# Attention and mixture-of-experts block on one core: down products turned round, transposes on VectorE, preparation jobs in other slots

## Chip, core and metric

One NeuronCore of a Trainium2 chip runs the whole kernel as a single program. The metric is the device time of one execution in microseconds (us). Three executions of the kernel before gave 531.87, 533.58 and 533.83 us, a median of 533.58 us.

## What is computed

`x` and `ctx` are 4 batches of 512 tokens with 256 features, all float32.

```python
x = x + tanh(g_xattn) * xattn(layernorm(x), ctx, ctx)     # 16 heads of 64, rope, window of 64
x = x + tanh(g_ffn)   * ffn(layernorm(x))

def ffn(x, shared_up, shared_down, routed_up, routed_down, router_w):
    up_s   = einsum('th,seh->tse', xt, shared_up)                  # 2 shared experts, 128 wide
    shared = einsum('tse,she->th', gelu(up_s), shared_down)
    probs  = softmax(xt @ router_w.T)                              # 16 routed experts
    topk_p, topk_i = top_k(probs, 4)
    gate   = zeros_like(probs).at[arange, topk_i].add(topk_p)
    up_r   = einsum('th,reh->tre', xt, routed_up)
    act    = gelu(up_r) * gate[:, :, None]
    return shared + einsum('tre,rhe->th', act, routed_down)
```

The float32 products are made of three products each, of a high and a low part of either operand (hi by hi, hi by lo, lo by hi).

## The kernel before

**Two stages.** The first (to about 300 us) is attention over 64 chunks (one head of one batch each), the second is 72 experts: for each of the 4 batches the 2 shared and the 16 routed ones. Each engine has its own program, and semaphores join them. The order is written out: `steps` lists the jobs of each attention chunk, `after[n]` the jobs that every engine does behind expert `n` (n counts from 0 to 71, 18 per batch), and the last chunks (58 to 63) and the first experts are written by hand for each engine. In this text "slot e" is the place behind expert e of a batch.

**An expert.** PE makes the up product of expert n (`up`, six 512-wide matmuls into `ring[0]`, weights stationary) and then the down product of expert n - 2 (`down`, twelve matmuls 256 wide: for each of 4 blocks of 128 tokens the gated activations are stationary and the weights move). Between the two lies a chain: ACT applies gelu (`act_g`), DVE multiplies by the gate (`gated`, into `act_f`, two buffers), ACT rounds the result to its high part (`round_gated`, into `oTh`), DVE makes the low part (`rest_gated`, into `oTl`). In trace rows the shared buffers carry the names of their owners: `act_g` is `sneg`, `act_f` is `prob`, the broadcast gates are `arena`. ACT does in slot n: round expert n - 1, gelu of n, jobs. DVE does: low part of n - 1, gating of n, jobs. The high part of n waits for the down product of n - 2, which frees `oTh[n % 2]`. Sums stand in two PSUM banks, in turn `psS` and `ring[1]`, and are added to `x` by four instructions of 128x256 at the batch's end (`z`).

**Preparing the next batch** is spread over the slots of the present one: `stat` (DVE: mean and variance of x, then POOL: the power -0.5 and the shift), `norm_a` and `norm_b` (ACT: two instructions each), `xT` (PE: 8 transposes of the normalised x, ACT and DVE: high and low parts), `r` (PE: 16 matmuls 32 wide, DVE: logits), `rexp` (ACT), `pick_a`, `pick_b` (DVE: the four best), `gT` (PE: 4 transposes of the gates, DVE: copy), `spread` (SP: gates to DRAM and back, spread over 128 partitions, one DMA per expert). In batch 0 POOL also makes the low parts of the expert weights (`w`).

**The last heads.** PE's `transpose_probs(c)` waits until ACT has copied the transposed probabilities of c - 1 out of `psT`; ACT does that (`copy_transposed`) in one order with the exponentials of later heads (`softmax_numerator`).

```python
            def expert(n):                     # PE
                if n < N - 1:
                    up(n)
                ...
                if n >= 4:
                    down(n - 2)
```

## Time and profile before

| | us |
|---|---|
| median of three runs | 533.58 |
| lowest and highest run | 531.87, 533.83 |
| profiled execution, its own time | 532.48 |
| its span in the profile | 530.7 |
| PE busy (matmuls) | 514.7 (97%) |
| weight loads busy | 454.2 (86%) |
| DVE busy | 344.9 (65%) |
| ACT busy | 311.7 (59%) |
| POOL busy | 276.0 (52%) |

The profile shows the span of the program on the core; the execution's own time is 1.8 us longer. A matmul's row lasts longer than the distance to the next row, because matmuls overlap; what a matmul costs PE is that distance, from start to start. The granted clock is 0.9 or more in all 40 slices of the span.

### The profile page before, as it was taken

The numbers are of one execution on the slowest core, as the hardware profiler recorded it, in microseconds if no ns is written. First come the engines' busy times: TensorE is split into PE (matmuls) and PEld (weight loads), VectorE is DVE, ScalarE is ACT, GpSimd is POOL, SyncE is SP. The second block draws the span as 40 slices with busy tenths as digits, with TensorE's granted clock in tenths as the row PEclk, the third lists the DMA queues.
The fourth block names the chain that finished last, engine by engine and source line by source line (L and its number), as shares of the span: only waits on it lengthen the run. The fifth ranks groups of instructions, "written<-read, shape, count | busy, mean of one in ns | idle before, by whom it ended". The sixth has DMA issues, their size and how long they took to land.

```text
span 530.7 us, 13192 instructions
## 1 busy us (share of the span) xinstructions
PE 514.7 (97%) x4906; PEld 454.2 (86%) x4906; DVE 344.9 (65%) x1121; ACT 311.7 (59%) x861; POOL 276.0 (52%) x213
## 2 busy tenths in 40 slices
PE   9888999999999999999999899999999999999997
PEld 5777797889889988888889789988998999998996
DVE  6868867658675687667766747665656465645444
ACT  3467667475766567665776765664455445644442
POOL 4899998779887978997898325430100010000000
PEclk9999999999999999999999999999999999999999
DMA  7362324011031101220221046206300550045001
GB/s 253 96 173 60 76 59 143 15 36 38 11 105 36 38 1 37 58 55 15 63 57 46 13 156 245 81 1 214 147 1 1 174 186 1 1 142 219 1 1 40
DMA packets 21614, 41.03 MB, mean 77 GB/s; under 512 B 3056, under 2 KB 5360, under 8 KB 21552
## 3 DMA queue, kind: packets, MB, share of 16 engines
q1 hardware_dynamic: 21552, 40.20, 24.6%
q8 instruction: 39, 0.64, 0.5%
q14 instruction: 23, 0.19, 0.1%
HBM read 30.62 MB, written 2.23 MB: 62 GB/s over the span
## 4 chain that ended last, share of the span: by engine, by line
PE 75%; POOL 10%; DVE 6%; issue 5%; ACT 3%; DMA 1%; SPq 0%; DVEq 0%; POOLq 0%; ACTq 0%
PE ring L939 51%; PE psS L939 9%; PE psO L1140 5%; PE psS L1109 4%; PE psT L1121 4%; POOL arena L433 3%; POOL arena L435 2%; POOL prob L439 2%; DVE arena L724 1%; POOL wl L447 1%; POOL arena L426 1%; PE psT L1086 1%; DMA craw<-in_ctx 1%; ACT prob L585 1%; POOL arena L423 1%
## 5 line engine op out<-in xcount | busy, mean ns | idle before, releaser
L939 PE MATMUL ring<-xTh,wh 128*128 128x512 f32 x272 | 111.3, 409 | 1.6 <-DVE wl L795 1.4
L939 PE MATMUL ring<-xTl,wh 128*128 128x512 f32 x272 | 106.9, 393 | 0.0
L939 PE MATMUL ring<-xTh,wl 128*128 128x512 f32 x272 | 106.8, 393 | 0.0
L939 PE MATMUL ring<-wh,oTh 128*128 128x256 f32 x272 | 78.3, 288 | 2.0 <-POOL wl L447 0.8
L939 PE MATMUL ring<-wh,oTl 128*128 128x256 f32 x272 | 76.6, 282 | 0.0
L939 PE MATMUL ring<-wl,oTh 128*128 128x256 f32 x272 | 76.4, 281 | 0.0
L439 POOL TENSOR_TENSOR prob<-prob,rinv 128x512 f32<-128x512 f32 x64 | 68.1, 1065 | 15.1 <-DVE rinv L853 15.0
L782 DVE TENSOR_TENSOR oTl<-prob,oTh 128x512 fp32r<-128x512 f32 x64 | 45.5, 710 | 43.5 <-ACT oTh L531 43.3
L531 ACT ACTIVATE oTh<-prob 128x512 fp32r<-128x512 f32 x64 | 40.4, 631 | 55.6 <-PE ring L939 25.2
L774 DVE TENSOR_TENSOR prob<-sneg,arena 128x512 f32<-128x512 f32 x64 | 47.4, 741 | 26.4 <-ACT sneg L515 26.4
L515 ACT ACTIVATE sneg<-ring 128x512 f32<-128x512 f32 x72 | 42.9, 596 | 36.7 <-PE ring L939 36.2
L594 ACT ACTIVATE pT<-psT 128x512 f32<-128x512 f32 x64 | 38.0, 594 | 42.1 <-PE psT L1121 42.1
L939 PEld LDWEIGHTS ring<-xTh,wl 128*128 128x128 f32 x272 | 51.1, 188 | 11.6
L939 PEld LDWEIGHTS ring<-xTh,wh 128*128 128x128 f32 x272 | 51.1, 188 | 10.9 <-issue 2.4
L939 PEld LDWEIGHTS ring<-xTl,wh 128*128 128x128 f32 x272 | 51.2, 188 | 7.4 <-issue 0.2
L585 ACT ACTIVATE prob<-arena,nmax 128x128 f32<-128x128 f32 x128 | 49.8, 394 | 10.6 <-DVE nmax L843 10.6
L939 PEld LDWEIGHTS ring<-wh,oTh 128*128 128x128 f32 x272 | 51.1, 188 | 5.4 <-issue 2.2
L585 ACT ACTIVATE prob<-sneg,nmax 128x128 f32<-128x128 f32 x128 | 49.5, 391 | 10.5 <-DVE nmax L843 10.5
L939 PEld LDWEIGHTS ring<-wl,oTh 128*128 128x128 f32 x272 | 51.6, 190 | 1.6
L458 POOL TENSOR_TENSOR rstd<-vare,mhalf 128x4 f32<-128x4 f32 x8 | 9.6, 1196 | 83.3 <-DVE vare L693 83.3
L939 PEld LDWEIGHTS ring<-wh,oTl 128*128 128x128 f32 x272 | 51.0, 187 | 0.0
L435 POOL TENSOR_TENSOR arena<-arena 128x512 f32<-128x512 f32 x36 | 47.3, 1314 | 2.8
(118 smaller groups left out, 1247.9 us busy)
## 6 DMA issues: line engine op xcount, KB each, us to landing
arena<-gate_scratch SPq DMA_DIRECT2D x64, 256.0 KB, 6.3
raw<-in_e SPq DMA_DIRECT2D x18, 256.0 KB, 2.6
raw<-in_w SPq DMA_DIRECT2D x16, 256.0 KB, 3.4
arena<-arena SPq DMA_DIRECT2D x16, 256.0 KB, 3.1
arena<-arena SPq DMA_DIRECT2D x16, 192.0 KB, 3.5
out<-x SPq DMA_DIRECT2D x16, 128.0 KB, 6.0
x<-in_x SPq DMA_DIRECT2D x3, 512.0 KB, 4.1
craw<-in_ctx SPq DMA_DIRECT2D x3, 512.0 KB, 5.5
```

The source lines that it names most:

```text
L435: pool.tensor_tensor(dst, dst, part, ALU.add).then_inc(qk_rot[i], 1)
L439: pool.tensor_tensor(prob[:, c % BUFS, :, :], prob[:, c % BUFS, :, :], rinv[:, c % BUFS, :].unsqueeze(2).to_broadcast([P, TT, P]), ALU.mul ...
L515: act.activation(act_g[:, n % 2, :], ring[0][:, n % 2, :], ACT.Gelu).then_inc(f_gelu, 1)
L531: act.activation(gated_parts(n)[0], src[:, n % 2, :], ACT.Copy).then_inc(f_hi, 1)
L585: last = act.activation(prob[:, c % BUFS, t, :], sneg[c % BUFS][:, t, :], ACT.Exp, bias=nmax[:, c % 4, t:t + 1], scale=-1.0, accum_out=rsu ...
L594: act.activation(pT[:, c % 4, :, :], psT[:, :, :], ACT.Copy).then_inc(p_out, 1)
L774: dve.tensor_tensor(act_f[:, n % 2, :], act_g[:, n % 2, :], gate_bc[:, r, :], ALU.mult).then_inc(f_mul, 1)
L782: dve.tensor_tensor(lo, src[:, n % 2, :], hi.bitcast(F32), ALU.subtract).then_inc(f_lo, 1)
L939: last = pe.matmul(out, a, b, start=start and i == 0 and j == 0, stop=stop and i == n - 1 and j == 2, skip_group_check=check)
L1109: last = pe.matmul(psS[odd][e * W:(e + 1) * W, t, :], qT[rows, u % 2, h // 2, blk * W:(blk + 1) * W], kT[rows, u % 2, h // 2, blk * W:(blk ...
L1121: last = pe.transpose(psT[:, t, :], prob[:, c % BUFS, t, :], ident[:, :])
L1140: last = pe.matmul(psO[h * DH:(h + 1) * DH, blk * W:(blk + 1) * W], v[:, u % 2, t, head * DH:(head + 1) * DH], pT[:, (2 * p + h) % 4, t, e ...
```

## The change

1. **Down products.** The weights become stationary and the activations move: for each half of the 256 output features three matmuls 512 wide, six in place of twelve of 256. The sums thus stand with the features on the partitions and the tokens along the row. Therefore `z` needs x in the same layout: new jobs `back` turn the x of each batch into `x1T` by DVE's 32x32 transposes, four jobs per batch, each of four instructions (32 partitions, 256 elements each). The output is stored in this layout, and the host turns it.
2. **Normalised x of batches 2 and 3** is turned by DVE (four jobs `turn` of the same four instructions in slots 5 to 8), and its high and low parts come from SBUF (`xhi` in slot 9, `xlo` in slot 10). Batch 1 keeps PE's transposes.
3. **Logits**: the router weights become stationary, four matmuls 512 wide into 32 partitions in place of 16; DVE turns the result (four transposes of 128 elements).
4. **Gates**: DVE turns them (four transposes of 128 elements); PE's four transposes go.
5. **Slots**: `stat` from 4 to 3; `norm_a`, `norm_b` from 6 and 7 both to 4; `xT` of batch 1 from 9 to 7; `r`, `rexp`, `pick_a`, `pick_b` one later; `gT` stays at 15.
6. **gelu** of n no longer waits for the low part of n - 2 but for its gating; `act_f` has four buffers, and gating no longer waits for the rounding.
7. **Last heads**: ACT copies the transposed probabilities of 58 before the exponentials of 60, and so on; the PE, ACT and DVE orders of heads 59 to 63 and experts 0 to 3 change.

```diff
-            for e, kind in ((4, "stat"), (6, "norm_a"), (7, "norm_b"), (9, "xT"), (10, "r"), (11, "rexp"),
-                            (12, "pick_a"), (13, "pick_b"), (15, "gT")):
...
+            for e, kind in ((3, "stat"), (4, "norm_a"), (4, "norm_b")):
+                after[b * NE + e].append((kind, B + b + 1))
+            if b == 0:
+                after[7].append(("xT", B + 1))
+            else:
+                for quarter in range(4):
+                    after[b * NE + 5 + quarter].append(("turn", 4 * (b + 1) + quarter))
+                after[b * NE + 9].append(("xhi", b + 1))
+                after[b * NE + 10].append(("xlo", b + 1))
+            for e, kind in ((11, "r"), (12, "rexp"), (13, "pick_a"), (14, "pick_b"), (15, "gT")):
...
+        for b, slots in enumerate(((9, 11, 16, 17), (2, 11, 16, 17), (2, 11, 16, 17), (3, 5, 7, 9))):
+            for quarter, e in enumerate(slots):
+                after[b * NE + e].append(("back", 4 * b + quarter))
...
             def gelu(n):
                 act.wait_ge(up_pe, n + 1)
-                if n >= 2:
+                if n >= 2 and experts[n - 2][1] < NS:
                     act.wait_ge(f_lo, n - 1)
+                elif n >= 2:
+                    b, e = experts[n - 2]
+                    act.wait_ge(f_mul, b * NR + e - NS + 1)
...
+                if c == CLOSING - 1:
+                    copy_transposed(58)
                 softmax_numerator(c)
...
-            copy_transposed(58)
+            copy_transposed(59)
             softmax_numerator(61)
-            copy_transposed(59)
+            round_att(29)
             do(("rexp", 0))
-            round_att(29)
+            copy_transposed(60)
             softmax_numerator(62)
-            copy_transposed(60)
+            copy_transposed(61)
...
+            def turn(dst, src, a):
+
+                blocks = src[QUAD * a:QUAD * (a + 1), :, :].rearrange("p t (k c j) -> p t k c j", k=KC, c=4)
+                for c in range(4):
+                    to = dst[QUAD * c:QUAD * (c + 1), :, :].rearrange("p k (t a j) -> p t k a j", t=TT, a=4)
+                    last = dve.transpose(to[:, :, :, a, :], blocks[:, :, :, c, :])
+                return last
...
-                link(dve.tensor_copy(lex[:, :, :], by_parts[:, :, 0, :]))
-                link(dve.tensor_tensor(lex[:, :, :], lex[:, :, :], by_parts[:, :, 1, :], ALU.add))
...
+                for a in range(4):
+                    last = dve.transpose(logits[QUAD * a:QUAD * (a + 1), :, :], by_tokens[:, :, a, :])
+                link(last)
+                link(dve.tensor_tensor(lex[:, :, :], logits[:, :, 0:NR], logits[:, :, NR:], ALU.add))
...
-                for t in range(TT):
-                    half, at = t // 2, (t % 2) * D
-                    last = product(sums(b, half)[:, at:at + D],
-                                   [(hi[:, t * P:(t + 1) * P], lo[:, t * P:(t + 1) * P])],
-                                   [cols(i, D, D)], start=(e == 0 and t % 2 == 0), stop=(e == NE - 1),
-                                   check=True)
-                    last.then_inc(down_pe, 1)
+                for kc in range(KC):
+                    product(sums(b, kc), [cols(i, D + kc * P, P)], [gated_parts(n)], start=e == 0,
+                            stop=e == NE - 1, check=True).then_inc(down_pe, 1)
...
-                elif kind == "gT":
-                    pe.wait_ge(r_gate, n + 1)
-                    for t in range(TT):
-                        last = pe.transpose(two[0][0:NR, t * P:(t + 1) * P], gate[:, t, :], ident[:, :])
-                    last.then_inc(gT_pe, 1)
```

**Place 1: PE, one down product in the second stage.** Before (`psS<-wh,oTh` is a piece of the weights moving over stationary activations):

```order
L939 MATMUL psS<-wh,oTh 128x256 [waits f_lo]
L939 MATMUL psS<-wl,oTh 128x256
L939 MATMUL psS<-wh,oTl 128x256
L939 MATMUL psS<-wh,oTh 128x256
L939 MATMUL psS<-wl,oTh 128x256
L939 MATMUL psS<-wh,oTl 128x256
L939 MATMUL psS<-wh,oTh 128x256
```

That pattern goes on to twelve rows. With the change the whole down product is six rows, the next up product right behind it:

```order
L1001 MATMUL ring<-oTh,wh 128x512 [waits f_lo]
L1001 MATMUL ring<-oTl,wh 128x512
L1001 MATMUL ring<-oTh,wl 128x512
L1001 MATMUL ring<-oTh,wh 128x512
L1001 MATMUL ring<-oTl,wh 128x512
L1001 MATMUL ring<-oTh,wl 128x512
L1001 MATMUL ring<-xTh,wh 128x512 [waits f_gelu]
```

Its wait for `f_lo` stays in front of the first row.

**Place 2: ACT, normalising the next x in the third batch.** (`oTh<-prob` rounds an expert, `sneg<-ring` is its gelu, `xn<-x` normalises.) Before:

```order
L531 ACTIVATE oTh<-prob 128x512 [waits down_pe,f_mul]
L515 ACTIVATE sneg<-ring 128x512 [waits f_lo,up_pe]
L575 ACTIVATE xn<-x,shift,rstd 128x256 [waits xT_pe,ln_rstd]
L575 ACTIVATE xn<-x,shift,rstd 128x256
L531 ACTIVATE oTh<-prob 128x512 [waits down_pe,f_mul]
L515 ACTIVATE sneg<-ring 128x512 [waits f_lo,up_pe]
L575 ACTIVATE xn<-x,shift,rstd 128x256 [waits xT_pe,ln_rstd]
L575 ACTIVATE xn<-x,shift,rstd 128x256
L531 ACTIVATE oTh<-prob 128x512 [waits down_pe,f_mul]
```

With the change:

```order
L535 ACTIVATE sneg<-ring 128x512 [waits f_mul,up_pe]
L603 ACTIVATE xn<-x,shift,rstd 128x256 [waits xn_turned,xT_pe,ln_rstd]
L603 ACTIVATE xn<-x,shift,rstd 128x256
L603 ACTIVATE xn<-x,shift,rstd 128x256 [waits xn_turned,xT_pe,ln_rstd]
L603 ACTIVATE xn<-x,shift,rstd 128x256
L551 ACTIVATE oTh<-prob 128x512 [waits down_pe,f_mul]
```

All four normalising instructions now stand together, one slot behind `stat`, ahead of the rounding of expert 4.

**Place 3: DVE, slot 11 with the change** (`prob<-sneg,arena` gates expert 11, `craw<-psT` turns the logits, `pT<-x` is the job `back`):

```order
L812 TENSOR_TENSOR prob<-sneg,arena 128x512 [waits gate_in9,f_gelu]
L775 STREAM_TRANSPOSE craw<-psT 32x128 [waits r_pe]
L775 STREAM_TRANSPOSE craw<-psT 32x128 x3
L777 TENSOR_TENSOR lex<-craw 128x64 [waits dve_link]
L778 TENSOR_REDUCE lmax<-lex 128x4 [waits dve_link]
L779 TENSOR_TENSOR lex<-lex,lmax 128x64 [waits dve_link]
L765 STREAM_TRANSPOSE pT<-x 32x4x2x32 [waits z_out,y_out]
```

Before, the copy `lex<-psT` stood where the four transposes of the logits stand, and nothing stood where `pT<-x` (four instructions) does.

## Rows read from the trace of the kernel before

**Rows 1.** The page, busy time of each engine, share, instructions.
```profile
PE 514.7 (97%) x4906; PEld 454.2 (86%) x4906; DVE 344.9 (65%) x1121; ACT 311.7 (59%) x861; POOL 276.0 (52%) x213
```

**Rows 2.** Timeline of PE, an expert (start us, us, engine, line, op).
```profile
324.03 0.40 PE L939 MATMUL ring<-xTh,wh 128*128 128x512 f32 x1
...
325.43 0.28 PE L939 MATMUL psS<-wh,oTh 128*128 128x256 f32 x1
...
326.86 0.40 PE L939 MATMUL ring<-xTh,wh 128*128 128x512 f32 x1
```

**Rows 3.** Timeline of PE, eleven 512-wide products in a row in attention.
```profile
153.54 0.39 PE L939 MATMUL ring<-xTl,wh 128*128 128x512 f32 x1
...
156.06 0.60 PE L1121 MATMUL psT<-ident,prob 128*128 128x128 f32 x4
```

**Rows 4.** Timeline of PE, preparing batch 1: transposes of x, then the router product.
```profile
338.17 0.60 PE L1036 MATMUL psT<-ident,xn 128*128 128x128 f32 x4
...
338.96 0.48 PE L939 MATMUL ring<-xTh,wh 128*128 128x512 f32 x1
339.27 0.40 PE L939 MATMUL ring<-xTl,wh 128*128 128x512 f32 x1
...
341.86 0.20 PE L1086 MATMUL psT<-rw_parts,xTh 128*128 128x32 f32 x1
...
343.58 0.48 PE L939 MATMUL ring<-xTh,wh 128*128 128x512 f32 x1
```

**Rows 5.** Timeline of PE, a late down product and the transposes of the gates.
```profile
356.27 0.40 PE L939 MATMUL ring<-xTh,wl 128*128 128x512 f32 x1
...
356.87 0.38 PE L939 MATMUL psS<-wh,oTh 128*128 128x256 f32 x1 [0.21 <-DVE oTl L782]
...
358.40 0.60 PE L1095 MATMUL psT<-ident,gate 128*16 128x128 f32 x4
...
358.75 0.48 PE L939 MATMUL ring<-xTh,wh 128*128 128x512 f32 x1
```

**Rows 6.** Timeline of PE, the last heads.
```profile
298.75 0.63 PE L1121 MATMUL psT<-ident,prob 128*128 128x128 f32 x4 [1.07 <-ACT pT L594]
```

**Rows 7.** Timeline of DVE, shuffles of 1024 and 512 columns and what follows each.
```profile
279.51 1.33 DVE L724 STREAM_SHUFFLE arena<-ring 128x1024 f32<-128x1024 f32 x1
280.73 1.21 DVE L727 TENSOR_TENSOR arena<-ring,cos 128x1024 f32<-128x1024 f32 x1
...
283.94 0.76 DVE L724 STREAM_SHUFFLE arena<-ring 128x512 f32<-128x512 f32 x1
284.58 0.68 DVE L727 TENSOR_TENSOR arena<-ring,cos 128x512 f32<-128x512 f32 x1
```

**Rows 8.** Timeline of all engines, statistics of the next x.
```profile
378.64 1.40 DVE L686 BATCH_NORM_STATS2 stats<-x 128x6 f32<-128x256 f32 x4
...
380.22 0.60 ACT L515 ACTIVATE sneg<-ring 128x512 f32<-128x512 f32 x1 [0.70 <-PE ring L939]
...
380.64 0.68 DVE L782 TENSOR_TENSOR oTl<-prob,oTh 128x512 fp32r<-128x512 f32 x1
...
382.26 0.20 POOL L463 TENSOR_TENSOR shift<-nmean,rstd 128x4 f32<-128x4 f32 x1
...
383.55 1.08 ACT L575 ACTIVATE xn<-x,shift,rstd 128x256 f32<-128x256 f32 x2
```

**Rows 9.** Timeline of DVE, the first experts.
```profile
321.91 1.28 DVE L811 SCALAR_TENSOR_TENSOR x<-ring,tg,x 128x1024 f32<-128x1024 f32 x1
323.11 0.68 DVE L782 TENSOR_TENSOR oTl<-prob,oTh 128x512 fp32r<-128x512 f32 x1
323.71 0.68 DVE L774 TENSOR_TENSOR prob<-sneg,arena 128x512 f32<-128x512 f32 x1
...
329.86 1.78 DVE L774 TENSOR_TENSOR prob<-sneg,arena 128x512 f32<-128x512 f32 x1
```

**Rows 10.** Timeline of PE, the last down product.
```profile
525.55 0.39 PE L939 MATMUL ring<-wh,oTh 128*128 128x256 f32 x1 [0.29 <-DVE oTl L782]
```

More of the change, by code:

```diff
@@ L275, in released @@
                     "v": (v_out, n + 1), "y": (y_out, n + 1),
[L276 removed]
+                    "r": (r_sub, n + 1)}[kind]
         def fillings(u):
@@ L369, in store @@
             def store(b):
-                for t in range(TT):
-                    sp.wait_ge(z_out, TT * b + t + 1)
-                    sp.dma_start(out_d[b][:, t, :], x[:, b, t, :]).then_inc(out_done, 16)
+                for i in range(4):
+                    part = slice(i % 2 * (L // 2), (i % 2 + 1) * (L // 2))
+                    sp.wait_ge(z_out, 4 * b + i + 1)
+                    sp.dma_start(out_d[b][:, i // 2, part], z_of(b)[:, i // 2, part]).then_inc(out_done, 16)
             def do(job):
@@ L567, in do @@
                     act.activation(lexp[:, :, :], lex[:, :, :], ACT.Exp).then_inc(r_exp, 1)
+                elif kind == "xhi":
+                    X = side(B + n)
+                    act.wait_ge(xn_turned, 4 * (n - 1))
+                    act.wait_ge(up_pe, NE * (n - 1))
+                    act.wait_ge(r_pe, n - 1)
+                    act.activation(xTh[X][:, :, :], xnT, ACT.Copy).then_inc(xT_hi, 1)
                 elif kind in ("norm_a", "norm_b"):
@@ L821, in do @@
                 elif kind == "gT":
-                    dve.wait_ge(gT_pe, n + 1)
                     if n:
                         dve.wait_ge(gT_dram, 16 * n)
-                    dve.tensor_copy(gT, banks(job)[0][0:NR, :]).then_inc(gT_out, 1)
+                    by_tokens = gT.rearrange("p (t a j) -> p t a j", t=TT, a=4)
+                    for a in range(4):
+                        last = dve.transpose(by_tokens[:, :, a, :], gate[QUAD * a:QUAD * (a + 1), :, :])
+                    last.then_inc(gT_out, 1)
+                elif kind == "turn":
+                    b, a = divmod(n, 4)
+                    dve.wait_ge(ln_norm, B + b + 1)
+                    turn(xnT, xn, a).then_inc(xn_turned, 1)
+                elif kind == "xlo":
+                    X = side(B + n)
+                    dve.wait_ge(xT_hi, B + n + 1)
+                    dve.tensor_tensor(xTl[X][:, :, :], xnT, xTh[X][:, :, :].bitcast(F32),
+                                      ALU.subtract).then_inc(xT_lo, 1)
+                elif kind == "back":
+                    b, a = divmod(n, 4)
+                    dve.wait_ge(y_out, GROUPS * (b + 1))
+                    if b == 0:
+                        dve.wait_ge(oT_pe, CHUNKS // 2)
+                    else:
+                        dve.wait_ge(z_out, 4 * b)
+                    turn(x1T, x[:, b, :, :], a).then_inc(x1_turned, 1)
                 elif kind == "expert":
@@ L901, in _ @@
                 for job in jobs:
+                    if (c, job[0]) == (CLOSING - 2, "xT"):
+                        invert(CLOSING - 2)
                     do(job)
@@ L1081, in do @@
                     X = side(B + n)
-                    for t in range(TT):
-                        for kc in range(KC):
-                            for part in (xTh[X], xTl[X]):
-                                last = pe.matmul(two[0][:, t * 2 * NR:(t + 1) * 2 * NR],
-                                                 part[:, kc, t * P:(t + 1) * P],
-                                                 rw_parts[:, kc, :, :].rearrange("p a e -> p (a e)"),
-                                                 start=kc == 0 and part is xTh[X],
-                                                 stop=kc == KC - 1 and part is xTl[X])
-                    last.then_inc(r_pe, 1)
-                elif kind == "gT":
-                    pe.wait_ge(r_gate, n + 1)
-                    for t in range(TT):
-                        last = pe.transpose(two[0][0:NR, t * P:(t + 1) * P], gate[:, t, :], ident[:, :])
-                    last.then_inc(gT_pe, 1)
+                    for kc in range(KC):
+                        for part in (xTh[X], xTl[X]):
+                            last = pe.matmul(two[0][0:2 * NR, :], rw_parts[:, kc, :, :].rearrange("p a e -> p (a e)"),
+                                             part[:, kc, :], start=kc == 0 and part is xTh[X],
+                                             stop=kc == KC - 1 and part is xTl[X])
+                    last.then_inc(r_pe, 1)
             def scores(c):
```

110 lines of the change are left out of this document (53 added, 57 removed).

## The prediction

> **What bounds the kernel now.** I read first the busy shares: PE has work in 97% of the span, DVE in 65%, ACT in 59%, POOL in 52% [rows 1]. So PE's work is the bound, and the change is worth what it takes out of PE's row of starts, less every new wait put into it. Then I read PE's timeline from start to start. In the second stage an expert takes 324.03 to 326.86 = 2.83 us, of which the six wide up matmuls take 1.40 and the twelve narrow down matmuls 1.43 [rows 2]. 72 x 2.83 = 204 us, the greater part of the 230 us from the last heads to the end. Beyond that there are the preparations of the next batch on PE [rows 4, 5], one late down product [rows 5], and a wait in the last heads [rows 6].
>
> **Terms that leave PE.**
>
> (a) Down products. Eleven 512-wide matmuls in a row take 153.54 to 156.06, 2.52 us, 0.229 us each [rows 3]; inside an expert the six take 1.40, 0.233 each [rows 2]. An expert becomes twelve of them: 2.75 by the one, 2.80 by the other, 2.78 in between, so 0.05 us less than 2.83 [rows 2]. 72 x 0.054 = 3.9 us; the bounds are 72 x 0.03 = 2.2 and 72 x 0.08 = 5.8. The halved number of rows saves little, because a 256-wide matmul costs PE only 1.43 / 12 = 0.119 us [rows 2], about half of a 512-wide one. The Trainium skill (TensorE: Matmul & The Clock Gate, Back-to-back issue gap) gives N/2.4 + 2.5 ns for a lone matmul's gap; by it twelve of 256 cost 1.31 us and six of 512 1.295, and (a) would be an estimated 1.1 us in all. The measured steps of 0.119 and 0.229 to 0.233 lie above its 0.109 and 0.216, so the trace disagrees and decides the sum.
>
> (b) Router product, 4 times. Its sixteen narrow matmuls take 341.86 to 343.58 = 1.72 us, and the next 512-wide matmul behind such a block is slower by about 0.08 (338.96 to 339.27 is 0.31, against 0.23) [rows 4]. In their place stand four wide ones, 4 x 0.23 = 0.92. That is 0.88 each, 3.5 us.
>
> (c) Transposes of x for batches 2 and 3: 338.17 to 338.96 = 0.79, plus 0.08 [rows 4]; twice, 1.7 us.
>
> (d) Transposes of the gates, 4 times: 358.40 to 358.75 = 0.35, plus the 0.08 [rows 5]: 1.7 us.
>
> (e) Last heads. The transposes of chunk 59 wait 1.07 us for ACT's copy, which stood behind an exponential [rows 6]. The copy now comes first and is done while PE makes the logits, and the inversion that POOL's division waits for is moved up as well, so the wait goes. What is late next there is nothing I can find above 0.3 us; I take another 0.5 for smaller waits of the same kind. 1.6 us; from 0 (another engine is as late) to 2.5.
>
> Sum: 3.9 + 3.5 + 1.7 + 1.7 + 1.6 = 12.4 us.
>
> **What DVE takes on.** No transpose of DVE is in the trace. The nearest row is the shuffle: 1024 columns take 279.51 to 280.73 = 1.22 us to the next start and 512 take 0.64 [rows 7], so 1.13 ns per column and 0.06 fixed; 256 columns are then 0.35 us, 128 are 0.20. A `back` or `turn` job is 4 x 0.35 = 1.4 us. An expert costs DVE 2 x 0.60 = 1.2 us [rows 9], of PE's 2.78; 1.4 fits into what is left, 1.58. 16 `back` and 8 `turn` jobs are 34 us of DVE's time, all beside PE. The worst slot is 11: logits (4 x 0.20, then some 0.7 us of small steps) and `back`, 2.9 + 1.2 = 4.1 us, 1.3 more than a slot. The low part of that expert is due two experts later. Its chain (gelu, gating, rounding, low part, about 0.65 each with its hop) is normally done about 2 us before PE wants it, so 1.3 fits. The lower bound for a job is the 4 x 0.33 of the statistics of 256 columns (1.40 for four [rows 8]), the upper 4 x 0.64, the price of a shuffle twice as wide [rows 7]. I take 0.35, since the shuffle is the same kind of row. Four wide `z` additions stay four, and SP's DMAs keep their slots (the gates leave a little earlier, since PE's part of the way is gone); I cost both at nothing. If DVE's cover were gone, each us of lateness would go to PE.
>
> **What comes back as waits.**
>
> (f) `norm` in one slot. Statistics start at 378.64, and POOL's shift ends at 382.26 + 0.20, 3.8 us later [rows 8]. So far three slots lay between. Now ACT comes to the normalising right behind gelu of expert 4 (380.22 + 0.60 if `stat` stands one slot earlier [rows 8]) and must wait to 382.5. It then runs all four, twice 1.0 us [rows 8], to 384.5. Behind it on ACT stands the rounding of expert 4 (0.6), behind that DVE's low part (0.7), ready at about 385.9. PE had handed up 4 over some 0.2 before that gelu, at 380.0; down 2, up 5, down 3 and up 6 follow, 4 x 1.39, so it wants the low part at about 385.6. 0.35 us late, plus 0.1 for the slower first matmul after a wait: 0.45 in each of batches 1 and 2. In batch 0 it is worse: the last attention sum (1.20 us) stands directly ahead of `stat` on DVE [rows 9]. The low part of expert 3 comes out about 0.6 late, and that of 4 another 1.6: 2.3 us. Together 3.2 us.
>
> (g) POOL still makes weights' low parts up to slot 13 of batch 0. A DVE instruction beside it takes 1.78 in place of 0.68 us [rows 9], and it already made a down product late by 0.60 - 0.23 = 0.37 [rows 5]. With `back` twice in that stretch I add 0.5; bounds 0 and 2.
>
> (h) The very last down product waits for its chain anyway (0.29 idle before it [rows 10]), so the last two steps gain nothing: 0.1.
>
> Sum of waits: 3.8 us. Net 12.4 - 3.8 = 8.6 us. The profiled execution took 532.48 us, so 523.9; that execution lies 1.1 below the median 533.58 and inside the three runs (531.87 to 533.83). I forecast **524.0 us**, 1.8% below.
>
> **Rivals.**
>
> *The waits (f) and (g) don't come.* ACT's queue may recover, since gelu no longer waits for the low part and `act_f` has four buffers. For: PE's 2 us of lead over the chain. Against: ACT works in order and the arithmetic of (f) leaves nothing over. 12.4 - 0.1 off: 520.2 us.
>
> *Wide rows cost twice narrow ones, and the heads are late elsewhere.* (a) falls to nothing and (e) to 0: 523.9 + 3.9 + 1.6 = 529.4; (a) alone gone: 527.8. For: 0.119 x 2 is 0.238, hardly above 0.233 [rows 2]. Against: rows 3. This includes the case that the change does not do what it says, fewer rows but not less time.
>
> *Slower: DVE becomes the bound in the second stage.* If a 256-element transpose of 4-byte values costs 0.64 us, as a shuffle twice as wide does, a job is 2.56 us and a `turn` slot holds 1.2 + 2.56 = 3.8 against PE's 2.78. Four such slots follow each other in batches 1 and 2 (4 x 1.0 each, 8 us), slot 11 is then 3.2 us over instead of 1.3 (some 1.5 to 2 us shown on PE, 3 times, 5 us), and slots 16 and 17 follow each other in three batches (1 to 1.5 each, 4 us): 17 us, 523.9 + 17 = 541 us. It decides from about 0.40 us a transpose on (1.2 + 4 x 0.40 = 2.8), and at about 0.5 it eats the whole gain. For: no row shows a transpose; the blocks are filled and emptied. Against: the shuffle's 1.13 ns per column [rows 7]. The Trainium skill (VectorE: DVE Perf Modes, The three transpose paths) gives 311 ns for 128x128 of 2-byte elements; doubled for twice the columns that is an estimated 0.62 us and would give this rival. No run here shows it yet.
>
> **How the numbers follow.** Forecast with its own spread 522 to 526.5: 0.50. First rival: 0.16. Second: 0.20. DVE bound: 0.14, of which a mild form (0.4 to 0.5 us a transpose, 525 to 532) takes about 0.05 and the full form 0.09. The range 519.5 to 530.0 takes in the first two rivals and the bounds of (a), (e) and (g), and leaves out the full form and the far ends. 0.5% of 533.6 is 2.7 us, about what a measurement of this kernel can tell from no change. Faster by more than that (below 530.9): 0.50 + 0.16 + 0.19 = 0.85, less 0.01 for tails, plus nothing of the mild form: 0.84. Within: 0.06, the mild form and the far end of the second rival. Slower: 0.10.
>
> **What would show it.** An expert's step of 2.76 to 2.80 us; the logits at 0.9 us on PE; no wait of 1 us before the transposes of chunk 59; waits of PE for `oTl` near the fourth expert of batches 0, 1, 2 of about 2.3, 0.45, 0.45; a DVE transpose of 256 elements near 0.35 us from start to start. A transpose above 0.4 us, or an expert's step of 2.83, would prove me wrong.

## The result, and the profile after

The changed kernel took 530.89 us (median of 8 runs, 530.51 to 532.19) against 533.48 us (8 runs, 531.87 to 534.31) of the kernel before in the same session: a ratio of 0.9953, 95% interval 0.9942 to 0.9963. That is 2.6 us faster. The forecast was 524.0 us with a range of 519.5 to 530.0, so the time lies 0.9 us above the range. The profiled execution took 532.19 us (span 530.4, before 530.7), 1.3 above its median.

Not all of the 2.6 us is the change's doing. For 46 executions of the kernel before, taken beside the experiments, the record has TensorE's mean granted clock, as a share of full speed. In ten it is 0.999, and they took 532.06 to 532.77 us (median 532.2); in 25 it is 0.995 to 0.997 (median 533.5), in eleven 0.994 (median 535.0). A mean that is lower by 0.003 is, by an estimate from these numbers, some 3 us at half the clock (0.003 x 530 / 0.5). All eight executions of the changed kernel have 0.999 or 1.0. So against the kernel before at 0.999 it is 532.2 - 530.9 = 1.3 us faster, and the other 1.2 us or so of the 2.6 are the clock. This is an estimate too: for the eight executions behind 533.48 the record has no clock. The ratios to the kernel before that are given below hold that share too; the differences between the experiments and the changed kernel don't, but for e6 (told there).

The page of the changed kernel, its busy line (answers [rows 1]) and the shares of the chain that ended last:

```profile
PE 507.7 (96%) x4394; PEld 421.2 (79%) x4394; DVE 388.0 (73%) x1240; ACT 309.6 (58%) x859; POOL 276.1 (52%) x213
...
PE 58%; DVE 17%; POOL 11%; issue 8%; ACT 4%; DMA 1%; SPq 0%; DVEq 0%; POOLq 0%; ACTq 0%
```

PE's busy time fell from 514.7 to 507.7 us. But in the chain PE holds 58%, where the page of before has 75%, and DVE went from 6% to 17%. Work left PE, and DVE came into the chain in its place. PE's timeline shows an expert with nothing in its way (start, duration, engine; answers [rows 2]):

```profile
362.28 0.39 PE L1001 MATMUL ring<-xTh,wh 128*128 128x512 f32 x1
...
363.68 0.40 PE L1001 MATMUL psS<-oTh,wh 128*128 128x512 f32 x1
...
365.07 0.39 PE L1001 MATMUL ring<-xTh,wh 128*128 128x512 f32 x1
```

1.40 for up, 1.39 for down, 2.79 in all; the forecast was 2.78. The same timeline at the logits of batch 0 and at the last heads (answers [rows 4, 6]):

```profile
297.61 0.39 PE L1136 MATMUL ring<-xTl,rw_parts 128*32 128x512 f32 x1
297.84 0.60 PE L1164 MATMUL psT<-ident,prob 128*128 128x128 f32 x4
298.60 1.10 PE L1152 MATMUL psS<-arena 64*64 64x128 f32 x32 [0.16 <-DVE nmax L902]
...
301.80 0.47 PE L1001 MATMUL ring<-xTh,wh 128*128 128x512 f32 x1 [0.23 <-DVE lex L779]
```

The transposes of chunk 59 follow the four wide products of the logits at once; the wait of 1.07 us is gone, and what is late next is 0.16 and 0.23. And here is what came in its place, PE's late down products (answers [rows 5, 10]; in brackets the idle time before the row and who ended it):

```profile
327.12 0.39 PE L1001 MATMUL ring<-xTh,wl 128*128 128x512 f32 x1
328.96 0.50 PE L1001 MATMUL psS<-oTh,wh 128*128 128x512 f32 x1 [1.46 <-DVE oTl L820]
...
351.67 0.50 PE L1001 MATMUL psS<-oTh,wh 128*128 128x512 f32 x1 [1.16 <-DVE oTl L820]
...
383.72 0.51 PE L1001 MATMUL ring<-oTh,wh 128*128 128x512 f32 x1 [0.40 <-DVE oTl L820]
...
525.14 0.50 PE L1001 MATMUL ring<-oTh,wh 128*128 128x512 f32 x1 [0.32 <-DVE oTl L820]
```

327.12 to 328.96 is 1.84 us where the usual step is 0.23. To see all waits at once I list the distance from the start of one up product to the start of the next; each holds up n, the wait for the low part of expert n - 2, and down n - 2. The columns e5, e7, e3 are experiments told below.

| batch, up of slot | before | changed | e5 | e7 | e3 | what is in it |
|---|---|---|---|---|---|---|
| most of 72 | 2.83 | 2.78 | 2.78 | 2.83 | 2.78 | nothing else |
| 0, 5 | 2.83 | 3.42 | 3.43 | 3.34 | 2.79 | normalising |
| 0, 6 | 2.82 | 4.51 | 4.50 | 4.51 | 2.78 | normalising |
| 0, 13 | 2.83 | 4.22 | 3.40 | 2.83 | 2.78 | slot 11: logits and back |
| 0, 15 | 3.64 | 3.56 | 3.55 | 2.98 | 3.43 | pick beside POOL (and 0.35 of gates on PE: before) |
| 1, 6 | 2.82 | 3.46 | 3.23 | 3.14 | 2.78 | normalising |
| 1, 7 | 2.83 | 3.02 | 2.77 | 3.02 | 2.79 | turn of slot 5 |
| 1, 8 | 2.83 | 3.13 | 2.79 | 3.14 | 2.78 | turn of slot 6 |
| 1, 9 | 3.62 | 3.15 | 2.78 | 3.13 | 3.59 | turn of slot 7 (PE transposes: before, e3) |
| 1, 10 | 4.62 | 3.15 | 2.79 | 3.15 | 3.79 | turn of slot 8 (logits: before, e3) |
| 1, 11 | 2.91 | 3.70 | 3.70 | 3.76 | 2.79 | logits on PE, 0.92 |
| 1, 13 | 2.82 | 3.53 | 3.18 | 2.83 | 2.79 | slot 11: logits and back |

In the last column "slot 11" and the like name the slot whose jobs make the low part late; PE waits for it two steps behind. Batch 2 repeats batch 1 within 0.03. What stands above 2.78 and is no work of PE adds up in the changed kernel to 0.64 + 1.73 + 1.44 + 0.78 in batch 0 and 2.9 in each of batches 1 and 2 (0.11 of it in slot 15, which the table leaves out), 10.3 us; before it was about 0.7. DVE's timeline shows the `turn` slots (answers [rows 7]):

```profile
386.60 0.69 DVE L812 TENSOR_TENSOR prob<-sneg,arena 128x512 f32<-128x512 f32 x1
387.31 1.78 DVE L765 STREAM_TRANSPOSE pT<-xn 32x256 f32<-32x256 f32 x4
389.13 0.69 DVE L820 TENSOR_TENSOR oTl<-prob,oTh 128x512 fp32r<-128x512 f32 x1
389.74 0.69 DVE L812 TENSOR_TENSOR prob<-sneg,arena 128x512 f32<-128x512 f32 x1
```

Four transposes hold DVE from 387.31 to 389.13, 1.82 us or 0.455 each, not 0.35; and the first starts 0.71 behind the gating, where a wide instruction starts 0.61 behind (389.13 to 389.74). One slot of DVE is 386.60 to 389.74 = 3.14 us. PE's step in these slots is 3.13 to 3.15: DVE sets it. In batch 0's slot 11:

```profile
347.04 1.26 DVE L775 STREAM_TRANSPOSE craw<-psT 32x128 f32<-32x128 f32 x4
...
349.11 1.78 DVE L765 STREAM_TRANSPOSE pT<-x 32x256 f32<-32x256 f32 x4
350.92 0.69 DVE L820 TENSOR_TENSOR oTl<-prob,oTh 128x512 fp32r<-128x512 f32 x1
```

347.04 to 350.92 = 3.88 us beside the usual 1.2; the prediction had 2.9. The normalising in batch 1, all engines (answers [rows 8]):

```profile
376.48 1.40 DVE L715 BATCH_NORM_STATS2 stats<-x 128x6 f32<-128x256 f32 x4
377.79 0.60 ACT L535 ACTIVATE sneg<-ring 128x512 f32<-128x512 f32 x1 [0.56 <-PE ring L1001]
380.11 0.20 POOL L480 TENSOR_TENSOR shift<-nmean,rstd 128x4 f32<-128x4 f32 x1
380.34 2.08 ACT L603 ACTIVATE xn<-x,shift,rstd 128x256 f32<-128x256 f32 x4 [1.95 <-POOL shift L480]
382.33 0.61 ACT L551 ACTIVATE oTh<-prob 128x512 fp32r<-128x512 f32 x1
382.97 0.69 DVE L820 TENSOR_TENSOR oTl<-prob,oTh 128x512 fp32r<-128x512 f32 x1 [3.21 <-ACT oTh L551]
```

This is the chain of (f), place by place: ACT stands idle 1.95 us until the shift is there, and DVE 3.21 us until the rounding behind the normalising is done. The size has a second source: with the `back` job of slot 2 ahead of them, the statistics start at 376.48. In e7 below, which has no `back` jobs, the same step is 3.14 us, 0.31 above that kernel's 2.83 in place of 0.68 above 2.78.

### The profile page after: what moved, and what is told of

Same layout as the page of the kernel before. It is cut to its first block, busy times and chain, and to the rows that moved or that the text cites. A ratio compares the mean times of both kernels' runs of the same rounds, so it can differ in the third digit from the quotient of the medians.

```text
span 530.4 us, 12299 instructions
## 1 busy us (share of the span) xinstructions
PE 507.7 (96%) x4394; PEld 421.2 (79%) x4394; DVE 388.0 (73%) x1240; ACT 309.6 (58%) x859; POOL 276.1 (52%) x213
## 4 chain that ended last, share of the span: by engine, by line
PE 58%; DVE 17%; POOL 11%; issue 8%; ACT 4%; DMA 1%; SPq 0%; DVEq 0%; POOLq 0%; ACTq 0%
PE ring L1001 41%; PE psS L1001 5%; PE psO L1183 5%; DVE pT L765 4%; PE psS L1152 4%; PE psT L1164 4%; POOL arena L450 3%; DVE prob L812 3%; POOL arena L452 2%; DVE oTl L820 2%; POOL prob L456 2%; DVE arena L753 2%; POOL wl L464 1%; DMA craw<-in_ctx 1%; POOL arena L443 1%
## 5 line engine op out<-in xcount | busy, mean ns | idle before, releaser
L1001 PE MATMUL ring<-xTh,wh 128*128 128x512 f32 x272 | 109.7, 403 | 3.6 <-DVE xTl L735 1.7
L812 DVE TENSOR_TENSOR prob<-sneg,arena 128x512 f32<-128x512 f32 x64 | 46.2, 722 | 9.9 <-ACT sneg L535 9.9
L450 POOL TENSOR_TENSOR arena<-arena,sin 128x512 f32<-128x512 f32 x36 | 47.5, 1318 | 1.3 <-DVE arena L753 1.3
L440 POOL TENSOR_TENSOR arena<-arena,sin 128x1024 f32<-128x1024 f32 x14 | 34.0, 2427 | 25.0 <-DVE arena L753 25.0
L464 POOL TENSOR_TENSOR wl<-raw,wh 128x512 fp32r<-128x512 f32 x22 | 30.9, 1402 | 29.9 <-ACT wh L564 29.9
L753 DVE STREAM_SHUFFLE arena<-ring 128x512 f32<-128x512 f32 (+1 forms) x49 | 45.3, 924 | 0.2
L1164 PE MATMUL psT<-ident,prob 128*128 128x128 f32 x256 | 38.9, 274 | 5.0 <-POOL prob L456 5.0
L849 DVE SCALAR_TENSOR_TENSOR x<-ring,tg,x 128x1024 f32<-128x1024 f32 x16 | 20.5, 1280 | 28.7 <-PE ring L1001 28.7
```

The costliest lines, as they stand in the source:

```text
L450: link(pool.tensor_tensor(part, part, sin[:, :], ALU.mult))
L753: dve.stream_shuffle(swap[:, i, pairs, :], part, [(lane + QUAD // 2) % QUAD for lane in range(QUAD)]).then_inc(qk_swap[i], 1)
L812: dve.tensor_tensor(act_f[:, n % 4, :], act_g[:, n % 2, :], gate_bc[:, r, :], ALU.mult).then_inc(f_mul, 1)
L1001: last = pe.matmul(out, a, b, start=start and i == 0 and j == 0, stop=stop and i == n - 1 and j == 2, skip_group_check=check)
L1164: last = pe.transpose(psT[:, t, :], prob[:, c % BUFS, t, :], ident[:, :])
```

## The experiments

**e1: x of batches 2 and 3 turned on PE again** (the DVE jobs `turn`, `xhi`, `xlo` go, all else as changed).

```diff
-            for e, kind in ((3, "stat"), (4, "norm_a"), (4, "norm_b")):
+            for e, kind in ((3, "stat"), (4, "norm_a"), (4, "norm_b"), (7, "xT")):
                 after[b * NE + e].append((kind, B + b + 1))
-            if b == 0:
-                after[7].append(("xT", B + 1))
-            else:
-                for quarter in range(4):
-                    after[b * NE + 5 + quarter].append(("turn", 4 * (b + 1) + quarter))
-                after[b * NE + 9].append(("xhi", b + 1))
-                after[b * NE + 10].append(("xlo", b + 1))
...
```

> The changed kernel, with the normalised x of batches 2 and 3 turned on PE again (as in batch 1), all else kept. Theory A (DVE's jobs of four transposes take 1.8 us and not 1.4, so a slot with one takes 3.1 us against PE's 2.78, and four in a row come out as waits on PE, 0.35 to 0.5 us each, 1.35 per batch): the waits behind slots 5 to 8 go, 2.7 us, PE gets 1.7 us of transposes back: about 530.0 us. Rival B (those waits are the lag that ACT's queue keeps from the four normalising instructions in slot 4): the waits in slots 5 to 8 stay, PE's 1.7 us come on top: about 532.6 us.

Measured 530.50 us (529.87 to 531.08), ratio to before 0.9948 [0.9928, 0.9967]. The steps of slots 8 to 10 fall to 2.86, 2.79 and 2.78, that of slot 7 rises to 3.56 with PE's own transposes. The medians of e1 and of the changed kernel lie only 0.4 apart and their runs overlap, so it is these steps that decide: term (c), 1.7 us saved on PE, was paid for with 2.6 us in DVE's slots.

**e2: e1 with the normalising in two slots again** (`stat` 4, `norm_a` 6, `norm_b` 7, `xT` 9, the rest as in e1).

> e1_pe_xT with the statistics in slot 4, the two halves of the normalising in slots 6 and 7 and the transposes of x in slot 9, as before the change. Theory A: the late down products of experts 3 and 4 go (2.4 us in batch 0, 0.67 in batches 1 and 2, 3.7 together): 3.7 us less than e1, about 526.3 us. Rival B (the last attention sum and the statistics on DVE make them late, not the wait of ACT): at most the 1.3 us of batches 1 and 2 go, about 528.7 us.

Measured 527.02 us (526.88 to 527.87), ratio 0.9886 [0.9867, 0.9906], 3.5 us faster than e1. The waits of (f) were 0.64 + 1.73 + 0.68 + 0.67 = 3.7 us; all four are gone. The forecast 3.2 for (f) was nearly right. The edit moves the statistics, the normalising and the transposes together; that it is ACT's wait for the shift is read from the rows above and not tried apart. The slot that ACT's jobs share was worth more than everything that part 2 took from PE.

**e3: e2 with the `back` jobs away from the logits.**

```diff
-            for e, kind in ((11, "r"), (12, "rexp"), (13, "pick_a"), (14, "pick_b"), (15, "gT")):
+            for e, kind in ((10, "r"), (11, "rexp"), (12, "pick_a"), (13, "pick_b"), (15, "gT")):
...
-        for b, slots in enumerate(((9, 11, 16, 17), (2, 11, 16, 17), (2, 11, 16, 17), (3, 5, 7, 9))):
+        for b, slots in enumerate(((8, 14, 16, 17), (2, 8, 14, 16), (2, 8, 14, 16), (3, 5, 7, 9))):
```

> e2_norm_apart with the jobs that turn x back moved: in batch 0 to slots 8, 14, 16, 17, in batches 1 and 2 to 2, 8, 14, 16, and the logits and picks in slots 10 to 13 as before the change; gates stay in 15. Theory A (slot 11 holds the logits and a job at once, 5.3 us of DVE): the late down products behind slots 11 to 13 go, 1.4 + 0.8 in batch 0 and 0.9 in batches 1 and 2, some 3.5 us: about 522.8 us. Rival B (POOL's weights in batch 0 make DVE late whatever stands there, and single jobs of 3.1 us show as well): only 1 us, about 525.3 us.

Measured 524.49 us (524.13 to 524.73), ratio 0.9834 [0.9812, 0.9855]: 2.5 us less than e2, between the two forecasts. The column e3 of the table shows why: every wait behind slots 4 to 11 of batches 1 and 2 is gone, and some 1.8 us is left in batch 0 and at the start of batch 1 (steps 0, 10, then 0, 14 to 0, 16, and 1, 1; not all are in the table).

**e4: a shuffle of the same shape in place of each 256-element transpose** (x is no longer turned inside its blocks, so the values of `x1T` and of the x of batches 2 and 3 are other ones).

```diff
-                    last = dve.transpose(to[:, :, :, a, :], blocks[:, :, :, c, :])
+                    last = dve.stream_shuffle(to[:, :, :, a, :], blocks[:, :, :, c, :],
+                                              list(range(QUAD)))
```

> The changed kernel with each 32x32 transpose of a turn or back job replaced by a shuffle of the same shape that leaves the lanes where they are; the blocks are therefore not transposed. Theory A (a transpose doesn't overlap its neighbours, since its block is filled and emptied): a shuffle starts 0.35 us after the one before it, a job takes 1.4 us, the waits in slots 5 to 8 go and those behind slot 11 shrink: about 527 us. Rival B (the 32 partitions and the short strided runs cost it, whatever the operation): 0.44 us from start to start, and the time of the changed kernel, 530.9 us.

Measured 531.71 us (531.38 to 531.88), ratio 0.9964 [0.9952, 0.9977], no faster than the changed kernel; the rival's price of 0.44 us came. DVE's timeline of e4:

```profile
386.16 0.44 DVE L765 STREAM_SHUFFLE pT<-xn 32x256 f32<-32x256 f32 x1
386.52 0.00 DVE L765 LOAD_MASK_SELECT pT<-xn  x1
386.62 0.43 DVE L765 STREAM_SHUFFLE pT<-xn 32x256 f32<-32x256 f32 x1
```

A shuffle takes 0.46 from start to start here as well. The small instruction that loads its mask starts 0.36 behind, where my price 0.35 would have put the next one; the shuffle itself is held 0.10 longer, until its forerunner's row has ended (386.16 + 0.44 = 386.60). So it isn't the transposing that costs. The shuffles of [rows 7] read and write all 128 partitions. In `turn` each instruction writes another group of 32 partitions than the one before.

**e5: each transpose writes to the group of 32 partitions that it reads from.** Number, shape and order of the instructions stay; the blocks land in other places of `x1T` and `xnT`, so the x that is added at the end and the x of batches 2 and 3 are not the turned ones.

```diff
-                    to = dst[QUAD * c:QUAD * (c + 1), :, :].rearrange("p k (t a j) -> p t k a j", t=TT, a=4)
-                    last = dve.transpose(to[:, :, :, a, :], blocks[:, :, :, c, :])
+                    to = dst[QUAD * a:QUAD * (a + 1), :, :].rearrange("p k (t a j) -> p t k a j", t=TT, a=4)
+                    last = dve.transpose(to[:, :, :, c, :], blocks[:, :, :, c, :])
```

> The changed kernel with every transpose of a turn or back job writing to the same group of 32 partitions that it reads from; shape, count, slots and waits are those of the changed kernel, but the blocks land in the wrong place. Theory A (a DVE instruction whose input or output starts in another 32-partition group than that of the instruction ahead starts only when all ahead have ended): inside a job the second to fourth start 0.35 us after the one ahead instead of 0.455, the first and the instruction behind the job are still held, a job takes 1.5 us instead of 1.8, the waits in slots 5 to 8 all but go: about 528 us. Rival B (instructions on 32 partitions, or with short runs, never overlap): 0.455 us as before, 530.9 us.

Measured 526.31 us (526.05 to 527.05), ratio 0.9857 [0.9834, 0.9880], 4.6 us less than the changed kernel. DVE's timeline of e5:

```profile
386.30 0.69 DVE L812 TENSOR_TENSOR prob<-sneg,arena 128x512 f32<-128x512 f32 x1
387.01 1.42 DVE L765 STREAM_TRANSPOSE pT<-xn 32x256 f32<-32x256 f32 x4
388.46 0.69 DVE L820 TENSOR_TENSOR oTl<-prob,oTh 128x512 fp32r<-128x512 f32 x1
389.07 0.69 DVE L812 TENSOR_TENSOR prob<-sneg,arena 128x512 f32<-128x512 f32 x1
```

The four now take 387.01 to 388.46 = 1.45 us in place of 1.82: about 0.34 from start to start (1.42 less the last row's own 0.39, over three) instead of 0.455. A row now starts before its forerunner has ended; in the changed kernel a row lasts about 0.44 and the next one starts only when it has ended. The slot is 2.77 us, PE's step 2.78, and slots 5 to 8 show no wait at all. Slot 11 loses half of its own. So 4.6 of the 6.9 us by which the forecast was missed come back: 2.6 in the turn slots, 1.5 behind the three slots 11, 0.5 behind the normalising of batches 1 and 2. Their cause is an overlap between neighbouring DVE instructions of about 0.1 us, lost three times in each of 24 jobs, in slots that had no room for it. The start of a job's first row, 0.71 us behind the gating, is as late in e5 as in the changed kernel. The Trainium skill (VectorE: DVE Perf Modes, Two Vector instructions with no wait between them) says that an instruction whose input or output starts in another quadrant of partitions than the engine's last read or write is held until every earlier one has finished. By that rule the trace agrees: 0.455 held, 0.34 not held. The prediction did not weigh it.

**e6: the kernel before with the new order of the last heads alone** (part 7; on PE, ACT and DVE, as in the diff).

> The kernel before with the new order of the last heads alone (on PE, ACT and DVE), its own products, slots and transposes kept. Theory A: the 1.07 us wait of PE for the copied probabilities goes and 0.3 to 0.5 us of small ones: the kernel before less 1.6 us, about 531.9 us. Rival B (the order pays only together with the shorter logits and without PE's transposes of the gates): 533.5 us.

Measured 531.08 us (530.12 to 532.16), ratio 0.9944 [0.9922, 0.9966]: 2.8 us faster than before by the medians, with an interval of 1.8 to 4.2 us. The profiled execution, one of the slower of its six, shows only 0.5 us from the transposes of x of batch 0 to the up product of expert 4, because something else came in:

```profile
297.23 0.65 PE L1125 MATMUL psT<-ident,prob 128*128 128x128 f32 x4
297.81 1.83 PE L1113 MATMUL psS<-arena 64*64 64x128 f32 x32
299.57 1.98 PE L1144 MATMUL psO<-pT,arena 128*64 128x64 f32 x32
```

and in the windows of the same execution (busy time of each engine, then PE's granted clock, as a share of full speed):

```profile
296.00:298.00 2.00, 2.00 (x25) 1.83 (x28) 1.73 (x13) 1.73 (x9) 0.00 (x0) 1.00 0.00 0
298.00:300.00 2.00, 2.00 (x40) 1.67 (x37) 1.13 (x5) 2.00 (x9) 1.04 (x1) 0.50 0.00 0
300.00:302.00 2.00, 2.00 (x35) 1.88 (x32) 1.05 (x9) 0.45 (x2) 1.04 (x1) 0.64 0.00 0
```

The same two blocks take 1.10 and 1.15 in the traces of before and of the changed kernel; here the granted clock is at its lower level (1.2 GHz) for about 3 us, and they take 1.83 and 1.98, 1.56 us more. Without that the trace gives 0.5 + 1.6 = 2.1 us for the order alone. The six times agree: three have a mean clock of 1.0 and took 530.12, 530.16 and 530.45 us, three have 0.996 or 0.997 and took 531.70 to 532.16. The first three lie some 2.0 us below the 532.2 of the kernel before at 0.999. By the same reckoning the whole change is worth 1.3 us, less than this one part of it.

**e7: the change without part 1** (narrow down products, no `back` jobs, `z` and stores as before; parts 2 to 7 as changed).

> The changed kernel without its first part: the down products narrow as before the change (twelve of 256), no back jobs, the sums and the stores in the old layout; all else as changed. Theory A (the 3.9 us that the wide products give are all but eaten by the back jobs on DVE): PE gets 72 x 0.054 = 3.9 us more, the lateness behind slots 11 to 13 (3.0 us) goes: about 531.5 us. Rival B (the back jobs cost nothing that shows, and the whole lateness is of the turn jobs and the normalising): 534.8 us.

Measured 528.92 us (528.38 to 529.32), ratio 0.9903 [0.9883, 0.9923]. Both forecasts said slower than the changed kernel; it is 2.0 us faster. Part 1, the greatest term of the sum, made the changed kernel slower. The turn slots of e7, PE first and then DVE:

```profile
386.78 0.39 PE L996 MATMUL ring<-wh,oTh 128*128 128x256 f32 x1
...
389.92 0.39 PE L996 MATMUL ring<-wh,oTh 128*128 128x256 f32 x1
```

```profile
386.64 0.68 DVE L809 TENSOR_TENSOR prob<-sneg,arena 128x512 f32<-128x512 f32 x1
387.36 1.78 DVE L762 STREAM_TRANSPOSE pT<-xn 32x256 f32<-32x256 f32 x4
...
389.78 0.68 DVE L809 TENSOR_TENSOR prob<-sneg,arena 128x512 f32<-128x512 f32 x1
```

3.14 us again, on both engines. Where DVE sets the pace, a cheaper down product buys nothing. The waits of e7 above its 2.83 add up to about 5.2 us, those of the changed kernel to 10.3; the 5.1 between them came in with part 1, against 3.1 us that PE saves. Most of it are the `back` jobs (1.4 + 2 x 0.75 behind slots 11 alone); in the turn slots it is only that 3.14 stays 3.14 while PE's own step is shorter.

**e8: e3 with batch 0's first `back` in slot 5 instead of 8.**

> e3_spread_back with the first back job of batch 0 in slot 5 instead of 8, away from the logits. Theory A (batch 0's 1.4 us of late down products behind slots 10 to 13 are due to DVE's backlog, which this job begins): 0.5 us less, 524.0 us. Rival B (they are due to POOL's weights, beside which DVE's instructions take 1.78 us instead of 0.69, and to ACT's table load): no change, 524.5 us.

Measured 525.75 us (525.33 to 526.73), ratio 0.9847 [0.9823, 0.9870], 1.3 us slower than e3, against both forecasts. The steps of batch 0 that differ: slot 12 takes 3.62 (e3 2.79), slot 14 takes 3.55 (3.05), slot 10 3.78 (3.90). What happens in slot 12 is shown with e10.

**e9: e3 without part 1.**

> The slots of e3 without part 1: down products narrow as before, no back jobs, z and the stores as before; x of all batches turned on PE, the normalising in two slots, logits and gates on DVE. Theory A: part 1 takes 72 x 0.054 = 3.9 us out of PE, and where DVE has room (e3) only about 1.5 us of that is given back in waits (350 to 357 us of e3's timeline), so this kernel is some 2 to 2.5 us slower than e3's 524.5: about 526.5 us. Rival: part 1 is worth nothing even then, because a narrow row costs in long stretches what half a wide one does: 524.5 us or less.

Measured 527.23 us (526.84 to 527.38), ratio 0.9883 [0.9864, 0.9903], 2.7 us slower than e3. Where DVE has room, part 1 is worth that much. The step of an expert is 2.825 against 2.78, so it takes 0.045 x 70 = 3.1 us out of PE. From the last up product to the end of the span it is 12.0 us in e3 and 11.6 in e9; the changed kernel has 11.7 with the same wide products, so where this 0.4 comes from stays open. Theory A holds, the rival is out.

**e10: e3 with batch 0's first `back` behind POOL's work** (14, 16, 17 and slot 0 of batch 1).

> e3 with the four back jobs of batch 0 in slots 14, 16, 17 and in slot 0 of the next batch (before: 8, 14, 16, 17), out of the stretch in which POOL still makes low parts, and one in the slot of a shared expert, where DVE has no gating. Theory A: the job in slot 8 is what makes the down products at 349.9 and 353.3 us late (0.15 and 0.56 us), so 0.7 us goes: 523.8 us. Rival: those waits come from the gating beside POOL and the logits, whatever DVE did in slot 8: 524.5 us, no change.

Measured 525.61 us (525.18 to 526.69), ratio 0.9858 [0.9834, 0.9882], 1.1 us slower than e3, again against both forecasts. e8, e9 and e10 share the new wait in slot 12 of batch 0. The timeline of e10 there:

```profile
342.17 1.35 POOL L457 TENSOR_TENSOR wl<-raw,wh 128x512 fp32r<-128x512 f32 x1 [2.30 <-ACT wh L557]
342.29 1.78 DVE L811 TENSOR_TENSOR oTl<-prob,oTh 128x512 fp32r<-128x512 f32 x1
...
344.13 0.50 PE L992 MATMUL psS<-oTh,wh 128*128 128x512 f32 x1 [0.58 <-DVE oTl L811]
```

and of e3 two slots and more earlier, where a `back` job meets POOL's work, and behind it a low part and POOL's next instruction start almost together:

```profile
333.38 1.40 POOL L457 TENSOR_TENSOR wl<-raw,wh 128x512 fp32r<-128x512 f32 x1 [1.11 <-ACT wh L557]
333.54 1.77 DVE L756 STREAM_TRANSPOSE pT<-x 32x256 f32<-32x256 f32 x4
...
335.35 0.69 DVE L811 TENSOR_TENSOR oTl<-prob,oTh 128x512 fp32r<-128x512 f32 x1
335.37 1.82 POOL L457 TENSOR_TENSOR wl<-raw,wh 128x512 fp32r<-128x512 f32 x1 [0.59 <-ACT wh L557]
```

The low part takes 0.69 us if it starts 0.02 ahead of POOL's instruction, which then takes 1.82, and 1.78 if POOL's started 0.12 ahead. The transposes beside POOL take their usual 1.77. So in batch 0 an idle DVE is no gain by itself: taking the job out of slot 8 moved a later low part, which in e3 takes 0.68, to where POOL is ahead. The Trainium skill (SBUF — State Buffer, Who interferes with whom) says that a DVE instruction with two SBUF inputs contends with a GpSimd instruction that reads SBUF, that the order in which they issue decides who blocks, and that a DVE instruction with one SBUF input does not contend. By that rule the trace agrees: 1.78 against 0.68 for the low part, 1.82 against 1.40 for POOL's instruction, and 1.77 for the four transposes beside it.

**e11: e3 with batch 0's last `back` in slot 0 of batch 1** (8, 14, 16, 18), **e12: also the second in slot 11** (8, 11, 16, 18).

> e3 with the fourth back job of batch 0 moved from slot 17 to slot 0 of the next batch, where DVE has no gating (8, 14, 16, 18). Theory A: two back jobs in neighbouring slots behind the gates' transposes are what makes e3's down product at the start of batch 1 late by 0.39 us; alone it fits, so 0.4 us goes and nothing upstream moves: 524.1 us, the step of the second expert of batch 1 back to 2.79. Rival: the wait moves along with the job, because the slots of the shared experts also hold z (4 wide additions): 524.5 us, no change.

> e11 with the second back job of batch 0 moved from slot 14 to slot 11, in which DVE only has low part and gating (8, 11, 16, 18). Theory A (in batch 0 it is chance which DVE instruction meets one of POOL's low parts and takes 1.78 instead of 0.68 us; every job moved ahead of POOL's last one shifts the whole sequence): e11's waits of 0.27, 0.65 and 0.36 us change places, their sum lands between 0.6 and 3 us, most likely no better than e11: 524 to 526 us. Rival: only the slot's own load counts; 1.2 + 1.8 = 3.0 us in slot 11 costs 0.2, slot 14 gets 0.3 free: 524.0 us.

Measured 524.16 us (524.01 to 525.08), ratio 0.9821 [0.9800, 0.9841], and 523.93 us (523.78 to 524.42), ratio 0.9814 [0.9794, 0.9834]. The step of slot 1 in batch 1 falls from 3.17 to 2.76 in e11, and that of slot 16 in batch 0 from 3.14 to 2.78 in e12: each of these two waits went. The times differ by less: the runs of e3, e11 and e12 overlap (e3 up to 524.73, e12 down to 523.78), while in their traces the stretch from the transposes of x of batch 0 to the end shortens from 231.5 to 231.2 to 230.7 us. In e12 the theory of the shifting sequence, 524 to 526 us, missed: up to slot 15 all steps stay as they were. The rival, the slot's own load, gave the right time, though the 0.2 us that it charged for slot 11 doesn't show (the step two behind it is 2.77). e12 is the lowest median found, 1.9% below the kernel before (1.6% below its 532.2 at clock 0.999); the order of the heads, the router product, gates and wide down products are those of the change, x is turned on PE.

## Why the prediction was wrong

**The step that failed** is "256 columns are then 0.35 us, 128 are 0.20. A `back` or `turn` job is 4 x 0.35 = 1.4 us". The four took 1.82 us, 0.455 each, and 0.1 more ahead of the first (slot 3.14 us); those of 128 elements took 0.32 each. The prediction named the point from which DVE decides itself ("from about 0.40 us a transpose on"), and with 0.455 the mild form of the third rival came true, 525 to 532 us, to which it gave 0.05. The 0.64 us of its full form, and the estimate of 0.62 beside it, were too high. The row was read rightly and used wrongly: the shuffle's neighbours work on the same partitions, the next transpose writes to others (e4, e5), and where it doesn't it costs 0.34, close to the 0.35 of the sum. My "against" for that rival was the very row that didn't show the case.

**Point by point.**

- (a) 3.9 us forecast, 3.1 measured (0.045 us an expert, e9 beside e3). Mis-sized a little; in the changed kernel itself the term was worth less than nothing, since its `back` jobs brought 5.1 us of waits (e7).
- (b) 3.5: right in batches 1 and 2. The step with the logits and the one behind it were 4.62 + 2.91 before and are 3.79 + 2.79 in e3, 0.95 less, of which 0.09 is the cheaper expert twice: 0.86 each.
- (c) 1.7 taken off PE and paid back by the turn slots (e1). The line "1.4 fits into what is left, 1.58" failed: 3.14 - 1.2 = 1.9 had to fit. The turn slots cost 0.24 + 0.35 + 0.37 + 0.37 = 1.3 us in either batch, 2.6 in all.
- (d) 1.7: right. In e7 the step of batch 1 that held the gates fell from 3.18 to 2.82 and the one behind it from 2.91 to 2.83, 0.44 each.
- (e) 1.6 forecast. From the transposes of x of batch 0 to up of expert 4 it was 29.88 us before and 27.28 after; less 0.88 and 0.43 of (b) and (d) and 0.15 of (a), 1.1 us for the order. By itself (e6) it was worth 2.1. So the parts do not simply add up here: with the order at 2.1, the others bring 0.5 in this stretch and not 1.46. New idle times of 0.16 and 0.23 us stand there (the row of 298.60 above, and the first up product at 301.80, behind the logits); the rest is open. The wait of 1.07 went, as said.
- (f) 3.2 forecast, 3.7 measured (2.37 in batch 0, where 2.3 was forecast; 0.67, not 0.45, in the others). Mechanism and place were right (e2). In batches 1 and 2 the sum left out the `back` job of slot 2, without which the wait is 0.31 (e7, which has the narrow down products as well).
- (g) 0.5 forecast. Slot 11 of batch 0 alone was 1.44, and slot 15 stood at 0.78 where 0.45 was already there. In batches 1 and 2 slot 11 cost 0.75 each and was costed at nothing: "so 1.3 fits" failed, DVE was 5.1 us in that slot and not 4.1. e5 takes it to 0.40, e3 to nothing.
- (h) right, 0.32 idle before the last down product, before 0.29.

Together: of the 12.4 us of gains 3.1 + 3.5 + 1.7 + 1.8 + 1.1 = 11.2 came, but the waits were 10.3 - 0.7 = 9.6 us and not 3.8. The 5.8 between are the turn slots, 2.6, slot 11 in three batches, 2.9, slot 15, 0.3, and 0.5 of (f), less the 0.5 of (g). The net 1.6 agrees with the two profiled executions, which take 239.4 and 237.9 us from the transposes of x of batch 0 to the end, and with the 1.3 us between the changed kernel and the kernel before at clock 0.999. That the medians lie 2.6 apart is the clock, as estimated above. What the changed kernel's profiled execution took above its median stands ahead of that stretch: the transposes start at 292.49, in all other versions between 290.6 and 291.8.

## What to carry to other kernels

A price read from a row holds for what its neighbours do as well: on VectorE ask whether the next instruction starts in the same group of 32 partitions, before you count on the overlap. When work moves off the bound engine, add up the receiving engine slot by slot, not as a mean (DVE is 73% busy here and still sets the pace in 11 slots), and keep jobs that lengthen the same chain in different slots. And where a part brings both a gain and a load, run the change without it: the greatest term of this sum was the one that made the kernel slower, until its jobs were spread. A median of a few executions can also carry a share of the clock: compare the granted clocks before a difference of 1 or 2 us is put down to an edit.

## What the runs showed of the hardware

- A DVE instruction on 32 partitions by 256 elements of 4 bytes costs 0.34 us from start to start when it writes to the same group of 32 partitions as its neighbour (e5), and 0.455 when it writes to another (changed kernel); a shuffle costs 0.46 in the second case (e4).
- Which of DVE and POOL pays in a collision is settled by about 0.1 us of starting time (e3, e10), so that taking load off DVE can cost 0.8 us (e8, e9, e10).
- PE's granted clock fell to its lower level (1.2 GHz) for about 3 us in one execution of e6, from 298 us on. PE had been busy for 2.00 of the 2.00 us before, with the last of sixteen router matmuls 32 wide and four transposes, and had last stood idle for 0.25 us at 295.2; the kernel before waits 1.07 us just there. It is no rare event: 36 of 46 executions of the kernel before and 3 of 6 of e6 have a mean clock of 0.997 or less. The other twelve versions, all with four wide router matmuls in place of the sixteen, have 0.998 or more in all of their 66 executions. Whether it is these matmuls that bring the fall wasn't tried. In e8 and e9 the lower level shows once each in the last microseconds, where PE has no work left.
